# Expert routing spread over the units of the shared expert, and layer-norm moments taken one batch ahead, in a two-layer attention and expert kernel

## Chip, cores and metric

One core of one Trainium2 chip. The metric is the time of one execution in microseconds on the device; the kernel before has a median of 3525.72 us over 3 runs (3525.45 to 3530.16).

## What is computed

The input `x` is 8 batches of 512 tokens of 256 numbers (4096 tokens in all). Each of two layers adds a cross attention and an expert layer to it:

```python
x = x + L0_xattn(_layernorm(x), ctx)
x = x + L0_ffn(_layernorm(x))            # 16 routed experts of 128, 1 shared expert
x = x + L1_xattn(ctx, _layernorm(x))
x = x + L1_ffn(_layernorm(x))            # 8 routed experts of 352, a shared expert of 2 x 352
# L0 choice of experts
scores = sigmoid(x @ gate_w.T); c = scores + e_bias
group_scores = top_k(c.reshape(T, 4, 4), 2).sum(-1)      # the best 2 of 4 groups stay
topk_idx = top_k(where(group kept, c, 0), 4)
w = scores[topk_idx]; w = w / (w.sum(-1) + 1e-20) * 2.5
# L1 choice
scores = softmax(x @ gate_w.T); w, i = top_k(scores, 2); w = w / (w.sum(-1) + 1e-20) * 2.5
# each expert e: y += w_e * (silu(x @ Wg_e) * (x @ Wu_e)) @ Wd_e ; the shared expert has weight 1
```

## The kernel before, in words

All engines run in order through a list of stages; between two stages stands a barrier of all engines. The residual `res` stays in SBUF. The stages, with their place in the profiled span: layer-0 attention (first its norms and transposes, 0 to 57 us, then its heads, to 261); logits and choice of layer 0 (261 to 338); experts of layer 0 (339 to 920); keys and attention of layer 1 (to 2837); logits and choice of layer 1 (2837 to 2896); slot plan (2897 to 2917); first half of layer 1's shared expert, named `ea` (2918 to 3054); routed blocks (3055 to 3381); second half of the shared expert, `eb` (3383 to the end).

**Norm and logits** (`moe_routes`, L546). For each of 8 batches VectorE runs `ln_vector` (L96): four `bn_stats`, four `bn_aggr`, the variance plus eps; it waits for ScalarE's square root, takes the reciprocal and writes four tiles `xh`. TensorE turns `xh` into PSUM `px`; ScalarE copies it to `xs` and rounds it into the high part of `XH`; GpSimd subtracts for the low part; TensorE multiplies `xs` with the gate weights into `pl`. TensorE turns batch b+1 before it does the logits of batch b. `ln_vector` of batch b+1 comes whole after that of batch b. The first stage of attention 0 uses the same `ln_vector`, for batch b+1, ahead of the copy of `px` of batch b (L195 to L199); there ScalarE's queue has the square root of b+1 (`ln_scalar`, L115) ahead of its copy of the context `cT`, after which GpSimd loads a further context tile, and SyncE loads batch b+2 of `x` once `xh` of batch b is written.

**Choice** (`route0` L696, `route1` L1042). When all logits are there, VectorE alone works: it ranks the experts of each token by comparing each pair (`chosen`, L657: for each distance d a comparison, an addition and a subtraction), takes those of low rank and weighs them into `Wt` (`weigh`, L677). In layer 1 a plan follows as a stage of its own (`layer1_plan`, L1098): two small matmuls count the tokens of each expert, VectorE works out a slot for each token and choice (`slot`), and the expert of each block (`bexp`).

**Experts** (`moe_experts`, L764). The work is a row of units: one unit is one batch and one piece of up to 128 of an expert's inner width. In layer 0 there are 17 experts of 8 units, in `ea` and `eb` 24 units (three pieces for each batch). Unit u: TensorE does `gate_up` (12 matmuls into `pG` and `pU`, L855), ScalarE the silu (L907), VectorE the product `mult` (L956), ScalarE rounds it to `hs` high (L910), GpSimd subtracts for `hs` low (L935), TensorE does `down` (12 matmuls, L871), and after a batch's last piece VectorE adds the result, times the token's weight, to `res` (`add`, four instructions, L965). TensorE's order is gate_up(u+1), down(u); VectorE's is mult(u+1), add(u). `pG` and `pU` have two buffers: gate_up(u+2) waits for mult(u). In layer 0 the loop runs over pairs of experts, 0 to 15, then the shared expert comes as expert 16, written out. In `ea` GpSimd also issues, after each unit's subtraction, three indirect DMAs that send the tokens' rows to their slots (`Dispatch`, L1188): 64 in all, so in units 0 to 21. The stage ends when all of them have landed.

Of the kernel before, what the change touches and what calls it, by code (L numbers as in the profile page):

```python
# [6 lines left out]
P = 128  # L7
B, S, D = 8, 512, 256
TPB = S // P
# [86 lines left out]
def ln_vector(dve, s, n, src, st, mv, ve, rs, dst):  # L96

    for t in range(TPB):
        dve.bn_stats(st[:, t, :], src(t)).then_inc(s["stats"], 1)
    dve.wait_ge(s["stats"], n * TPB + TPB)  # L100
    dve.memset(ve[:, :], 0.0).then_inc(s["cleared"], 1)
    for t in range(TPB):
        dve.bn_aggr(mv[:, t, :], st[:, t, :]).then_inc(s["moments"], 1)
    dve.wait_ge(s["moments"], n * TPB + TPB)
    dve.wait_ge(s["cleared"], n + 1)
    dve.tensor_scalar(ve[:, :], mv[:, :, 1], EPS, None, ALU.add).then_inc(s["var"], 1)
    dve.wait_ge(s["sd"], n + 1)
    dve.reciprocal(rs[:, :], ve[:, :]).then_inc(s["rstd"], 1)
    dve.wait_ge(s["rstd"], n + 1)
    for t in range(TPB):  # L110
        dve.tensor_scalar(dst(t), src(t), mv[:, t, 0:1], rs[:, t:t + 1], ALU.subtract,
                          ALU.mult).then_inc(s["xhat"], 1)


def ln_scalar(act, s, n, ve):  # L115
    act.wait_ge(s["var"], n + 1)
    act.activation(ve[:, :], ve[:, :], ACT.Sqrt).then_inc(s["sd"], 1)
# [14 lines left out]
def layer0_attention(nc, io, res, ident):  # L132
    with ExitStack() as ctx:
# [5 lines left out]
        with ExitStack() as inner:  # L139
# [4 lines left out]
            st = sb1("a_st", [P, TPB, 6])  # L144
            mv = sb1("a_mv", [P, TPB, 2])
            ve = sb1("a_ve", [P, TPB])
            rs = sb1("a_rs", [P, TPB])
# [7 lines left out]
            with nc.Block() as block:  # L155
# [30 lines left out]
                def _(dve):  # L186
                    for k in range(2):
                        dve.memset(ahead[:, k:k + 1], 0.0).then_inc(x_out, 1)
                    def normalise(b, i, k):
                        dve.wait_ge(x_in[k], 16 * i + 16)  # L190

                        ln_vector(dve, ls, b, lambda t: res[:, bass.ds(b * TPB + t, 1), :].rearrange(
                            "p a d -> p (a d)"), st, mv, ve, rs, lambda t: xh[:, k, t, :])

                    def emit(b, i, k):  # L195
                        if not (isinstance(b, int) and b == B - 1):
# [4 lines left out]
                    normalise(0, 0, 0)  # L201
# [3 lines left out]
                def _(act):  # L205
                    for k in range(2):
                        act.copy(ahead[:, 2 + k:3 + k], ident[:, 0:1]).then_inc(c_out, 1)
                    def emit(b, i, k):
                        if not (isinstance(b, int) and b == B - 1):
                            ln_scalar(act, ls, b + 1, ve)  # L210
# [3 lines left out]
                    ln_scalar(act, ls, 0, ve)  # L214
# [331 lines left out]
def moe_routes(nc, io, res, ident, XH, Wt, tag, E, route, rows=None):  # L546


    with ExitStack() as ctx:
# [4 lines left out]
        st = sb(f"{tag}_st", [P, TPB, 6])  # L554
        mv = sb(f"{tag}_mv", [P, TPB, 2])
        ve = sb(f"{tag}_ve", [P, TPB])
        rs = sb(f"{tag}_rs", [P, TPB])
# [7 lines left out]
        r = route(nc, io, sb, sem, pl, Wt, logits_done, tag)  # L565

        with nc.Block() as block:
            @block.sync
            def _(sp):
                sp.dma_start(gate[:, :, :], io[f"{tag}_gate"]).then_inc(gate_in, 16)  # L570
                r["sync"](sp)

            @block.vector
            def _(dve):
                def emit(b, i, k):
                    if not (isinstance(b, int) and b < 2):
                        dve.wait_ge(turned, b - 1)
                    ln_vector(dve, ls, b, lambda t: res[:, bass.ds(b * TPB + t, 1), :].rearrange(
                        "p a d -> p (a d)"), st, mv, ve, rs, lambda t: xh[:, k, t, :])

                for_batches(dve, emit)
                r["vector"](dve)

            @block.gpsimd
            def _(pool):
                r["gpsimd_first"](pool)
# [12 lines left out]
            def _(act):  # L599
# [3 lines left out]
                def emit(b, i, k):  # L603
                    if not (isinstance(b, int) and b == B - 1):
                        ln_scalar(act, ls, b + 1, ve)
# [9 lines left out]
                ln_scalar(act, ls, 0, ve)  # L615
                for_batches(act, emit)
                r["scalar"](act)
# [39 lines left out]
def chosen(dve, c, v, E, top, beats, rank, sel):  # L657

    v3, r3 = (x.rearrange("p (g e) -> p g e", e=E) for x in (v, rank))


    for e in range(E):
        n = c.done(dve.memset(r3[:, :, e:e + 1], float(E - 1 - e)))
    G = v3.shape[1]
    for d in range(1, E):
# [1502 lines left out]
```

## Time and profile before

| | |
|---|---|
| runs, median (lowest, highest) | 3525.72 us (3525.45, 3530.16) |
| the profiled execution's own time | 3523.55 us |
| its span, first to last instruction | 3522.0 us |
| busy in the span: TensorE, VectorE | 3188.7 us (91%), 2037.6 us (58%) |
| busy: ScalarE, GpSimd | 1273.8 us (36%), 1626.9 us (46%) |
| mean granted TensorE clock | 0.945 of full speed |

PE is TensorE, PEld its weight loads, DVE VectorE, ACT ScalarE, POOL GpSimd, SP SyncE; a q behind a name is that engine's queue of instructions, which issues DMAs and waits. The stages follow each other, so each has its own limit, and a busy share over the whole span says little of one stage.

### The profile page before, as it was taken

To read this page: it belongs to the slowest core of one execution; us is meant where nothing else is said; L and a number is where in the kernel's file an instruction comes from. 1 tells how busy PE (TensorE), PEld (TensorE's weight loads), DVE (VectorE), ACT (ScalarE), POOL (GpSimd) and SP (SyncE) were. 2 spreads that over 40 slices of the span, in tenths; PEclk is the share of its full clock that TensorE was granted. 3 is DMA by queue.
4 is the path that set the end of the run, shared out by engine and by line. 5 is a ranking of instruction groups with operands and counts; after the bars stand their busy time and mean duration, and the time that the engine had idled before them with its cause. 6 is when DMAs were issued, how large, how long until landed. Compare 5 with 4: busy or idle time off the path is not lost. (4 is left out here: it accounts for less than half of the span.)

```text
span 3522.0 us, 56185 instructions
## 1 busy us (share of the span) xinstructions
PE 3188.7 (91%) x17981; PEld 2290.7 (65%) x17982; DVE 2037.6 (58%) x4470; ACT 1273.8 (36%) x1786; POOL 1626.9 (46%) x933
## 2 busy tenths in 40 slices
PE   5875999999539999999999999999999957699988
PEld 4655888888536666666666666666666555477766
DVE  5656555555746666666766766666666662122235
ACT  2332333333434444444444444444444432122222
POOL 5002333333235666655666655666656636500037
PEclk8995999999769999999999999999999958899999
DMA  4000000001451111111111101111010031421223
GB/s 110 1 1 9 14 13 9 13 9 57 162 214 46 52 45 46 53 45 35 61 45 54 45 27 69 45 54 45 27 69 28 7 106 64 140 68 63 63 70 109
DMA packets 89978, 192.94 MB, mean 55 GB/s; under 512 B 12768, under 2 KB 58152, under 8 KB 83760
## 3 DMA queue, kind: packets, MB, share of 16 engines
q1 hardware_dynamic: 74864, 162.28, 13.1%
q0 software_dynamic: 10816, 21.07, 2.1%
q10 hardware_dynamic: 4224, 8.65, 0.7%
q8 instruction: 40, 0.66, 0.1%
q14 instruction: 34, 0.28, 0.0%
HBM read 137.60 MB, written 54.30 MB: 54 GB/s over the span
## 5 line engine op out<-in xcount | busy, mean ns | idle before, releaser
L2070 POOL TENSOR_TENSOR d_acc<-d_acc,d_pr 128x1024 f32<-128x1024 f32 x384 | 938.2, 2443 | 91.1 <-ACT d_pr L1974 60.4
L1974 ACT ACTIVATE d_pr<-d_p 128x1024 f32<-128x1024 f32 x512 | 487.0, 1026 | 236.2 <-PE d_p L1909 236.2
L1843 PE MATMUL d_pO<-d_pr,d_V 128*64 128x512 f32 x2048 | 473.0, 599 | 0.0
L2070 POOL TENSOR_TENSOR d_acc<-d_pr 128x1024 f32<-128x1024 f32 x64 | 153.1, 2392 | 620.9 <-ACT d_pr L1974 620.9
L2019 DVE TENSOR_REDUCE d_nm<-d_p 128x2 f32<-128x1024 f32 x256 | 304.6, 1222 | 94.9 <-PE d_p L1886 94.9
L2014 DVE CUSTOM_DVE_ANT_0 d_biased<-d_p,d_masked 128x512 f32<-128x512 f32 x512 | 330.6, 688 | 31.8 <-issue 31.8
L935 POOL TENSOR_TENSOR e_hs<-e_hf,e_hs 128x512 fp32r<-128x512 f32 x136 | 175.6, 1291 | 365.4 <-ACT e_hs L910 365.4
L1843 PEld LDWEIGHTS d_pO<-d_pr,d_V 128*64 128x64 f32 x2048 | 135.4, 136 | 261.5 <-issue 235.0
L965 DVE SCALAR_TENSOR_TENSOR res<-e_pY,m_Wt,res 128x256 f32<-128x256 f32 x544 | 225.9, 478 | 44.6 <-PE e_pY L871 43.8
L2030 DVE RECIPROCAL d_rb<-d_rb 128x128 f32<-128x128 f32 x256 | 224.6, 920 | 7.5 <-ACT d_rb L1967 7.5
L871 PEld LDWEIGHTS e_pY<-e_Wd,e_hs 128*128 128x128 f32 x1632 | 213.5, 191 | 13.8 <-POOL e_hs L935 2.2
L871 PE MATMUL e_pY<-e_Wd,e_hs 128*128 128x256 f32 x1632 | 217.2, 283 | 2.7 <-POOL e_hs L935 2.7
L855 PE MATMUL e_pG<-m_XH,e_Wgu 128*128 128x512 f32 x816 | 212.1, 395 | 3.6 <-issue 3.6
L956 DVE TENSOR_TENSOR e_hf<-e_sl,e_pU 128x512 f32<-128x512 f32 x136 | 93.7, 689 | 208.9 <-ACT e_sl L907 208.9
L1886 PE MATMUL d_p<-d_KH,d_QH 64*128 64x512 f32 x1024 | 208.1, 443 | 5.4 <-DVE d_nm L2014 2.5
L1886 PEld LDWEIGHTS d_p<-d_KH,d_QH 64*128 64x128 f32 x1024 | 88.8, 184 | 190.3 <-issue 127.9
L1959 ACT COPY d_V<-d_p 128x1024 f32<-128x1024 f32 x64 | 64.8, 1012 | 400.1 <-PE d_p L1874 400.1
L1909 PE MATMUL d_p<-d_QM,d_KM 64*128 64x512 f32 x1024 | 208.3, 402 | 0.2 <-ACT d_pr L1974 0.2
L855 PE MATMUL e_pU<-m_XH,e_Wgu 128*128 128x512 f32 x816 | 208.3, 391 | 0.0
L1909 PE MATMUL d_p<-d_QH,d_KL 64*128 64x512 f32 x1024 | 202.3, 390 | 0.0
L1909 PE MATMUL d_p<-d_QL,d_KH 64*128 64x512 f32 x1024 | 202.0, 389 | 0.0
L1909 PE MATMUL d_p<-d_QH,d_KH 64*128 64x512 f32 x1024 | 201.6, 388 | 0.0
(287 smaller groups left out, 5628.2 us busy)
## 6 DMA issues: line engine op xcount, KB each, us to landing
d_W<-w_split SPq DMA_DIRECT2D x32, 1536.0 KB, 6.4
kv_split<-c_ys SPq DMA_DIRECT2D x16, 1024.0 KB, 5.7
d_kv<-kv_split SPq DMA_DIRECT2D x8, 2048.0 KB, 10.6
d_masked<-mask_bias SPq DMA_DIRECT2D x64, 256.0 KB
x_slots<-m_zeros SPq DMA_DIRECT2D x1, 9088.0 KB, 29.7
b_x<-x_slots SPq DMA_DIRECT2D x71, 128.0 KB, 2.0
y_slots<-b_y SPq DMA_DIRECT2D x71, 128.0 KB, 1.7
w_split<-w_parts SPq DMA_DIRECT2D x4, 1536.0 KB, 5.3
```

The lines of the kernel that those rows point to most:

```text
L855: last = pe.matmul(out[u % 2][0:fw, :], lhsT, XH[:, xp, k, n * S:(n + 1) * S], start=start, stop=(k == DC - 1 and (wp, xp) == PASSES[-1]))
L871: last = pe.matmul(pY[n % 2][:, t, :], hs[0:fw, u % 2, hp, t * P:(t + 1) * P], Wd[j][0:fw, wp, f, :], start=(f == 0 and m == 0 and t % 2 = ...
L935: pool.tensor_tensor(hs[0:fw, u % 2, LO, :], hf[0:fw, u % 2, :], hs[0:fw, u % 2, HI, :].bitcast(F32), ALU.subtract).then_inc(lo_done, 1)
L965: dve.scalar_tensor_tensor(res[:, tile, :], pY[n % 2][:, t, :], Wt[:, tile, bass.ds(e + column, 1)], res[:, tile, :], ALU.mult, ALU.add).t ...
L1843: last = pe.matmul(pO[own[h], :], V[vb][:, s, par * P + h * HD1:par * P + (h + 1) * HD1], pr[:, s % PT, h, :], start=(s == 0), stop=(s == ...
L1886: last = pe.matmul(out[:, h, :], QH[j][own[h], qt * P:(qt + 1) * P], KH[j][own[h], m * S:(m + 1) * S], start=True, stop=True)
L1909: last = pe.matmul(out[:, h, :], k_[own[h], s * P:(s + 1) * P], q_[own[h], :], start=(i == 0), stop=(i == len(terms) - 1))
L1974: act.activation(pr[:, n % PT, :, :], slot(st, what, n)[:, :, :], ACT.Exp).then_inc(exp_done, 1)
L2014: dve.tensor_tensor_reduce(biased[:, h, :], out[:, h, :], masked[j][:, :], -1.0, MASKED, ALU.add, ALU.min, nm2[:, j, h * TPB + qt, m:m + 1 ...
L2019: dve.tensor_reduce(both, out[:, :, :], AX.X, ALU.max, negate=True).then_inc(max_done, 1)
L2030: dve.reciprocal(rb[:, quarter], rb[:, quarter]).then_inc(r_done, 1)
L2070: pool.tensor_tensor(acc[:, q, :, :], a, pr[:, s % PT, :, :], ALU.add).then_inc(acc_done, 1)
```

## The change

Four edits.

1. **Norms.** `ln_vector` is split into `ln_moments` (to the variance) and `ln_apply` (reciprocal and tiles), with two buffers. In both logits stages VectorE takes the moments of batch b+1 ahead of the application to batch b. In attention 0 the order is: moments of b+1, copy of `px` of b, application to b+1.
2. **Choice of layer 0.** The logits stage ends with the sigmoid. The experts' stage begins with the shared expert (`last_first`), written out, and behind each of its 8 units VectorE runs one piece of the ranking; the weights are done after unit 7. The loop then runs over the routed experts.
3. **Choice and plan of layer 1.** The logits stage ends with a copy of the logits to SBUF. Choice and plan stand as eleven pieces behind units 0 to 10 of `ea`. The exponential is run by ScalarE behind unit 1, the counts by TensorE behind unit 4, in the `pG` and `pU` buffers of that unit; gate_up(6), which writes these next, waits until they are read. The stage of the plan is gone.
4. **`ea`.** The low part of `hs` is made by VectorE, ahead of `mult` (`low_on_vector`). GpSimd waits once for the slots, which are there after unit 8, and issues the 64 indirect DMAs; its list has no other wait.

The core of the diff (`chosen` is cut into `rank_begin`, `rank_steps` and `rank_end` with the same instructions):

```diff
-def ln_vector(dve, s, n, src, st, mv, ve, rs, dst):
+def ln_moments(dve, s, n, k, src, st, mv, ve):
     (bn_stats, memset, bn_aggr, variance + EPS, as before, in buffer k)
+def ln_apply(dve, s, n, k, src, mv, ve, rs, dst):
     dve.wait_ge(s["sd"], n + 1)
     (reciprocal and the four tiles, as before, from buffer k)
@@ attention 0, VectorE
-                            normalise(b + 1, i + k, 1 - k)
+                            moments(b + 1, i + k, 1 - k)
                         dve.wait_ge(x_turned, b + 1)
                         dve.tensor_copy(xT[:, :, bass.ds(b * S, S)], px[k][:, :, :]).then_inc(x_out, 1)
+                        if more:
+                            apply(b + 1, 1 - k)
@@ moe_routes, now moe_logits, VectorE
                 def emit(b, i, k):
+                    if not (isinstance(b, int) and b == B - 1):
+                        ln_moments(dve, ls, b + 1, 1 - k, tile_of(b + 1), st, mv, ve)
                     if not (isinstance(b, int) and b < 2):
                         dve.wait_ge(turned, b - 1)
-                    ln_vector(...)
+                    ln_apply(dve, ls, b, k, tile_of(b), mv, ve, rs, lambda t: xh[:, k, t, :])
+                ln_moments(dve, ls, 0, 0, tile_of(0), st, mv, ve)
                 for_batches(dve, emit)
-                r["vector"](dve)
@@ ScalarE, end of the stage
+                act.wait_ge(logits_done, B + 2)
+                route.take_logits(act, pl)
@@ moe_experts
-        tail = NX % 2 or 2
-        loops = (NX - tail) // 2
+        tail = (NX - 1) % 2 or 2
+        loops = (NX - 1 - tail) // 2
         def for_units(eng, emit):
+            for u in range(UPE):
+                emit(0, 0, u, NX == 1 and u == UPE - 1)
@@ TensorE: in gate_up, and behind down
+                    if isinstance(e, int) and e == 0:
+                        beside.spare_read(pe, u)
+                        beside.first_tensor(pe, u, (pG[u % 2], pU[u % 2]))
@@ GpSimd
-                    pool.wait_ge(hi_done, U + 1)
-                    pool.tensor_tensor(hs[0:fw, u % 2, LO, :], ...)
+                    if not low_on_vector:
+                        pool.wait_ge(hi_done, U + 1)
+                        pool.tensor_tensor(hs[0:fw, u % 2, LO, :], ...)
@@ VectorE
                 def emit(e, j, u, last):
+                    if low_on_vector:
+                        low(e, u)
                     if not last:
                         mult(*next_pair(e, j, u))
                     if u % NF == NF - 1:
                         add(e, u // NF)
                     beside.vector(...)
+                    if isinstance(e, int) and e == 0:
+                        beside.first_vector(dve, u, (pG[u % 2], pU[u % 2]))
@@ Route0.first_vector
+        if u == 0:     (bias, pair sums, their maximum, rank_begin of the groups)
+        elif u == 1:   (rank of the groups, mask, rank_begin)
+        elif u < B - 1:
+            ds = {2: range(1, 3), 3: range(3, 5), 4: range(5, 8), 5: range(8, 11), 6: range(11, E0)}[u]
+            rank_steps(dve, self.c, self.ch[:, :], self.rank[:, :], E0, self.beats, ds)
+        else:          (rank_end, weigh)
@@ Route1
+    SEND_FROM, SEND = 11, 5
+    COUNT_AT = 4
+    def take_logits(self, act, pl):
+        act.copy(self.lg[:, :], pl[:, :, :].rearrange("p t e -> p (t e)")).then_inc(self.taken, 1)
+    def first_tensor(self, pe, u, spare):
+        if u == self.COUNT_AT:
+            pe.wait_ge(self.pick_ready, 1)
+            (the two matmuls of the counts, into spare)
+    def spare_read(self, pe, u):
+        if u == self.COUNT_AT + 2:
+            pe.wait_ge(self.counts_read, 1)
+    def first_scalar(self, act, u):
+        if u == 1:
+            act.wait_ge(self.shifted, 1)
+            act.activation(self.lg[:, :], self.lg[:, :], ACT.Exp).then_inc(self.exp_done, 1)
+    def first_vector(self, dve, u, spare):
+        0: maximum, subtraction, constants   1: softmax, distances 1, 2   2: distances 3 to 7
+        3: rank_end, picked, weigh   4: counts, prefix sums   5: places, blocks of each expert
+        6: starts, number of the choice   7, 8: slot and weight of choice 0, 1 (slot_ready)
+        9, 10: expert of each block
+    def gpsimd(self, pool, u):
+        if u == self.SEND_FROM:
+            pool.wait_ge(self.slot_ready, 2)
+        if u >= self.SEND_FROM:
+            for _ in range(min(self.SEND, NT * TOPK1 - self.sent)):
+                (one indirect DMA, as before)
```

## Rows read from the trace of the kernel before

**Rows 1.** Windows by stage: start:end, us, busy (instructions) by engine, PEclk, DMA share, GB/s.
```profile
262.00:308.00 46.00, 40.90 (x196) 40.31 (x196) 31.74 (x119) 20.06 (x27) 19.95 (x16) 0.52 0.01 1
308.00:338.00 30.00, 0.00 (x0) 0.00 (x0) 27.61 (x89) 0.48 (x1) 0.00 (x0) 0.50 0.00 0
88.00:240.00 152.00, 134.72 (x562) 93.24 (x560) 97.95 (x174) 51.07 (x89) 0.00 (x0) 1.00 0.00 1
240.00:260.00 20.00, 12.78 (x40) 7.39 (x40) 7.04 (x14) 4.19 (x7) 0.00 (x0) 0.83 0.00 0
```

**Rows 2.** Timeline, logits stage of layer 0: start, duration, engine, line, operation, count [idle before].
```profile
261.40 1.41 DVE L99 BATCH_NORM_STATS2 m_st<-res 128x6 f32<-128x256 f32 x4 [0.92 <-PEq L86]
263.92 1.38 DVE L111 TENSOR_SCALAR m_xh<-res,m_mv,m_rs 128x256 f32<-128x256 f32 x4
...
269.16 1.97 PE L632 MATMUL m_px<-ident,m_xh 128*128 128x128 f32 x8 [1.82 <-DVE m_xh L111]
...
299.26 1.95 PE L632 MATMUL m_px<-ident,m_xh 128*128 128x128 f32 x8
...
301.00 6.85 PE L642 MATMUL m_pl<-m_gate,m_xs 128*128 128x16 f32 x32
```

**Rows 3.** Timeline, VectorE: first instruction of the choice of layer 0, first of its experts.
```profile
308.51 0.69 DVE L719 TENSOR_TENSOR m_ch<-m_sg,m_ebias 128x512 f32<-128x512 f32 x1 [11.31 <-ACT m_sg L713]
...
339.04 0.09 DVE L946 MEMSET e_ahead<- 128x1 f32 x2 [1.07 <-PEq L86]
```

**Rows 4.** Windows over what becomes pieces 0 and 7 of 8, layer 0.
```profile
308.50:311.60 3.10, 0.00 (x0) 0.00 (x0) 2.92 (x7) 0.00 (x0) 0.00 (x0) 0.50 0.00 0
...
334.54:338.00 3.46, 0.00 (x0) 0.00 (x0) 3.18 (x8) 0.00 (x0) 0.00 (x0) 0.50 0.00 0
```

**Rows 5.** Timeline, VectorE in the experts of layer 0: mult, add, mult.
```profile
357.83 0.69 DVE L956 TENSOR_TENSOR e_hf<-e_sl,e_pU 128x512 f32<-128x512 f32 x1 [1.50 <-ACT e_sl L907]
...
358.85 1.66 DVE L965 SCALAR_TENSOR_TENSOR res<-e_pY,m_Wt,res 128x256 f32<-128x256 f32 x4 [0.33 <-PE e_pY L871]
...
362.01 0.69 DVE L956 TENSOR_TENSOR e_hf<-e_sl,e_pU 128x512 f32<-128x512 f32 x1 [1.50 <-ACT e_sl L907]
```

**Rows 6.** Timeline, logits stage of layer 1: a GpSimd subtraction and a VectorE instruction beside it.
```profile
2846.84 2.50 POOL L594 TENSOR_TENSOR m_XH<-m_xs,m_XH 128x512 f32 x2 [8.89 <-ACT m_XH L613]
...
2847.16 0.97 DVE L106 TENSOR_SCALAR m_ve<-m_mv 128x4 f32<-128x4 f32 x1
```

**Rows 7.** Timeline, layer 1: table load, first instruction of the choice, first of `ea`.
```profile
2880.64 1.28 ACT L1063 ACT_TABLE_LOAD   x1
...
2884.21 0.42 DVE L1069 TENSOR_REDUCE m_tot<-m_pl 128x32 f32<-128x256 f32 x1 [9.60 <-PE m_pl L642]
...
2918.11 0.09 DVE L946 MEMSET ea_ahead<- 128x1 f32 x2 [1.18 <-PEq L86]
```

**Rows 8.** Window over what becomes piece 2 of layer 1.
```profile
2889.47:2893.44 3.97, 0.00 (x0) 0.00 (x0) 3.59 (x16) 0.00 (x0) 0.00 (x0) 0.50 0.00 0
```

**Rows 9.** Timeline, `ea`: second mult, two sends, the last send, first load of the blocks.
```profile
2936.16 0.69 DVE L956 TENSOR_TENSOR ea_hf<-ea_sl,ea_pU 128x512 f32<-128x512 f32 x1 [2.48 <-ACT ea_sl L907]
...
2961.05 0.99 POOL L1188 DMA_INDIRECT x_slots<-m_rows,m_slot  x1 [0.17 <-issue]
...
2962.34 0.97 POOL L1188 DMA_INDIRECT x_slots<-m_rows,m_slot  x1 [0.30 <-issue]
...
3041.27 0.99 POOL L1188 DMA_INDIRECT x_slots<-m_rows,m_slot  x1 [0.17 <-issue]
...
3055.65 28.95 SPq L1296 DMA_DIRECT2D b_x<-x_slots  x5
```

**Rows 10.** Timeline, first stage: load of batch 4, its first use, the last copy.
```profile
21.22 0.41 SPq L159 DMA_DIRECT2D res<-in_x_dram  x1
...
29.11 1.41 DVE L99 BATCH_NORM_STATS2 a_st<-res 128x6 f32 x4 [2.05 <-DMA res<-in_x_dram]
...
54.87 1.23 DVE L199 COPY a_xT<-a_px 128x1024 f32<-128x1024 f32 x1 [3.82 <-PE a_px L233]
```

More of the change, by code:

```diff
@@ L654, in over, with rank_begin, rank_steps @@
     return a.rearrange("p (o m) -> p o m", o=1).to_broadcast([P, n, a.shape[1]])
-def chosen(dve, c, v, E, top, beats, rank, sel):
+def rank_begin(dve, c, rank, E):
+    r3 = rank.rearrange("p (g e) -> p g e", e=E)
+    for e in range(E):
+        c.done(dve.memset(r3[:, :, e:e + 1], float(E - 1 - e)))
+def rank_steps(dve, c, v, rank, E, beats, ds):
     v3, r3 = (x.rearrange("p (g e) -> p g e", e=E) for x in (v, rank))
-    for e in range(E):
-        n = c.done(dve.memset(r3[:, :, e:e + 1], float(E - 1 - e)))
     G = v3.shape[1]
-    for d in range(1, E):
+    for d in ds:
+        dve.wait_ge(c.sem, c.now())
         b3 = beats[d % 2][:, 0:G * (E - d)].rearrange("p (g e) -> p g e", e=E - d)
@@ L689, in weigh @@
     dve.wait_ge(c.sem, n)
-    c.done(dve.memset(Wt[:, :, E:E + shared], 1.0))
     n = c.done(dve.tensor_tensor(Wt[:, :, 0:E], sel.rearrange("p (t e) -> p t e", e=E), over(tot, E, "last"),
@@ L912, in emit @@
                         split(e + 1, (j + 1) % 2)
+                    if isinstance(e, int) and e == 0:
+                        beside.first_scalar(act, u)
                     if isinstance(e, int) and e == NX - 1:
@@ new lines, in __init__ @@
+        TE = NT * E1
+        self.Wt, self.rows, self.slot, self.wk, self.bexp, self.xslots = Wt, rows, slot, wk, bexp, xslots
+        self.sent = 0
+        self.zeros = sb("m1_zeros", [P, D])
+        self.lg, self.sel, self.rank = (sb(f"m1_{n}", [P, TE]) for n in ("lg", "sel", "rank"))
+        self.beats = [sb(f"m1_beats{k}", [P, TE]) for k in range(2)]
+        self.total = sb("m1_tot", [P, NT])
+        self.upper = sb("s_upper", [P, P])
+        self.ones = sb("s_ones", [P, P])
+        self.order_i = sb("s_order_i", [P, NBLK], mybir.dt.int32)
@@ new lines, in __init__ @@
+        self.order_f = sb("s_order_f", [P, NBLK])
+        self.thr = sb("s_thr", [P, NT])
+        self.picked, self.tot, self.run, self.run2, self.place, self.mk = (
+            sb(f"s_{n}", [P, TE]) for n in ("picked", "tot", "run", "run2", "place", "mk"))
+        self.nblk, self.bs, self.bs2, self.start = (sb(f"s_{n}", [P, E1]) for n in ("nblk", "bs", "bs2", "start"))
+        self.bf = sb("s_bf", [P, NBLK])
+        self.slot_f = sb("s_slot_f", [P, TOPK1, NT])
+        (self.zeros_ready, self.slots_cleared, self.set_up, self.taken, self.shifted, self.exp_done, self.consts,
+         self.pick_ready, self.counted, self.counts_read, self.slot_ready, self.scattered, self.steps) = (
+             sem(f"s_{n}") for n in ("zeros_ready", "slots_cleared", "set_up", "taken", "shifted", "exp_done", "consts",
+                                     "pick_ready", "counted", "counts_read", "slot_ready", "scattered", "steps"))
@@ new lines, in before_vector, with take_logits, first_tensor @@
+    def before_vector(self, dve):
+        dve.memset(self.Wt[:, :, E1:E1 + NS1], 1.0).then_inc(self.set_up, 1)
+    def take_logits(self, act, pl):
+        act.copy(self.lg[:, :], pl[:, :, :].rearrange("p t e -> p (t e)")).then_inc(self.taken, 1)
+    COUNT_AT = 4
+    def first_tensor(self, pe, u, spare):
+        if u == self.COUNT_AT:
+            pe.wait_ge(self.pick_ready, 1)
+            for out, left in zip(spare, (self.upper, self.ones)):
+                pe.matmul(out[:, 0:NT * E1], left[:, :], self.picked[:, :], start=True, stop=True
+                          ).then_inc(self.counted, 1)
```

409 lines of the change are left out of this document (205 added, 204 removed).

## Prediction

> **What bounds the kernel now.** I read the windows by stage first. Where TensorE has work it is busy, but the two choices are holes: in 308 to 338 us it does nothing and VectorE works alone, 27.61 of 30 us [rows 1]. The timeline then gives the holes' edges: in layer 0 from the choice's first instruction (308.51) to the experts' first (339.04), 30.5 us [rows 3]; in layer 1 from 2884.21 to 2918.11, 33.9 us, plan and two barriers within [rows 7]. In the logits stages TensorE sets the pace: its turns come each (299.26 - 269.16)/6 = 5.02 us, and 40.9 of 46 us are busy, at a granted clock of 0.52 [rows 1, 2]. In layer 0's experts a unit takes 362.01 - 357.83 = 4.18 us; VectorE needs 0.69 + 1.66 = 2.35 of it, so 1.8 is free [rows 5]. In `ea` a unit takes (3041.27 - 2961.05)/16 = 5.01 us: three sends of 0.97 and a pause of 0.30 each on GpSimd, and a subtraction in the rest, 1.2, without a gap [rows 9]. There GpSimd bounds.
>
> **Choice of layer 0.** The stage now ends with the sigmoid, which ended at 308.5; a barrier takes 1.07 [rows 3]. The experts start at 309.6, 29.5 us earlier. The same instructions now stand behind the units: eight pieces, from 3.1 to 4.4 us, 29.5 together: the stretch between the edges without its barrier [rows 3], first and last of the eight in [rows 4]. VectorE's list per unit becomes 2.35 + 3.7 = 6.05 us against TensorE's 4.18. It is strictly in order and mult(u+2) stands behind piece u; gate_up(u+4) waits for that mult. So here VectorE bounds. Without the pieces mult(2) to mult(9) take 7 x 4.18 = 29.3 us. With them mult(2) waits for piece 0, some 2 us after its old place of 357.83, and each further cycle is piece + 2.4: the pieces of units 1 to 7 (26.4) and 7 x 2.4 = 16.8 bring mult(9) to 45.2 us after the old mult(2). Delay 45.2 - 29.3 = 16. TensorE's buffers give back almost nothing, since down(9) waits for the same mult. Added to this: VectorE's ranking reads two SBUF tiles, and a GpSimd subtraction of 1.3 us falls into each unit. A VectorE instruction that takes 0.17 elsewhere took 0.97 beside GpSimd, to the end of the first of two subtractions [rows 6]. Bounds per unit 0 and 1.3 us; most of the subtraction falls beside `add`, so I take 0.25, 2 us in all. Net: -29.5 + 16 + 2 = **-11.5**.
>
> The Trainium skill ("SBUF — State Buffer", on the shared port pair) says that a VectorE instruction with two SBUF inputs and a GpSimd instruction take an exclusive lock, and the loser waits to the other's end. By that rule alone, with no overlap by `add`, the 8 units would lose 8 x 1.3 = 10 us; the trace agrees that the wait ends with the other's end [rows 6].
>
> **Norms.** In the logits stages both engines' work stays, only the start differs. Moments take 2.0 us (263.92 - 261.40 less 0.5 for root and reciprocal), the application 1.6 [rows 2]. Batch 1's tiles are now there after three moments and two applications, 6.0 + 3.2 = 9.2: 270.6, against 269.1 before (turn(1) began at 269.16, waiting for VectorE). From there TensorE is never late, so 1.5 us stay, in both layers: **+3**. Bounds: 0, and a gain of 6 us per stage if TensorE should get its full clock and VectorE's list (3.9) be the pace.
> In attention 0 the order gets worse. Application b+1 stands behind the copy that waits for the turn of b. So ScalarE's root, and behind it the copy of the context, come an application (1.6 us) later, and the context load behind that; and `x` of batch b+2 is asked for later. That load takes 29.11 - 21.22 = 7.9 us and its user already waits 2.05 for it [rows 10]. The cycle over two batches becomes load 7.9, moments 2.0, copy 1.2, application 1.6 = 12.7. The first such application ends at 18.7 (turn of batch 0 to 15.9, copy 1.2, application 1.6); three cycles give 56.8, then turn and copy 3.2: 60, against 54.87 + 1.23 = 56.1 before, the stage's last copy [rows 10]. I take **+3**; bounds -1 (the roots' waits of 0.5 go) and +7.
>
> **Choice and plan of layer 1.** A copy of 0.42 us and one barrier replace 33.9 us: `ea` starts at 2885.75, 32.3 us earlier [rows 7]. All times now with this shift. Two mults are done at 2904.5 (2936.16 + 0.69 - 32.3) [rows 9]. Then VectorE's list up to the end of piece 8:
> - pieces 0 to 8: 1.85 + 24.1 = 26.0 (3.6, 3.97, 2.7, 3.6, 2.4, 2.7, 2.6, 2.6 for pieces 1 to 8, cut from the same stretch; the dearest, piece 2, in [rows 8]);
> - eight low parts of 0.73 and eight mults of 0.73: 11.7. No row shows the low part on VectorE; the nearest is the mult, 0.69; bounds 0.6 and 1.3 (GpSimd's time);
> - three adds, 5.0, and before each 0.75 for the down that the low part has just released: 2.2;
> - silu(2) behind an exponential that stands between two table loads of 1.28 [rows 7]: 1.6 late;
> - piece 4 waits for down(4) and the two count matmuls: 1.9; while they are read gate_up(6) waits, 0.1 more.
> Sum 48.5: the slots are there at 2953.0. TensorE (4.18 a unit) would then be through with all 24 units at about 3017. But GpSimd only now begins 64 sends of 1.27 = 81.7 us, and needs to 3034.7. So the sends set the end, 18 us behind TensorE. The last lands 2 us later, a barrier takes 2: first load of the blocks at 3038.7 against 3055.65 [rows 9]: -17. VectorE's low parts, two SBUF inputs each, run beside 19 units of sends; a send may be held by one (0 to 0.7 us per unit, 0 to 13 in all). I take 2: **-15**. What is late next is thus the DMA issue, not the plan. The idle TensorE starts the blocks at half clock, but it waits there for weights anyway.
>
> The pieces 9 and 10 (3 us) and the constants on GpSimd (0.8 us, now in the logits stage beside idle GpSimd) cost nothing: 14 units of slack on VectorE, and GpSimd is busy 19.95 of 46 us in a logits stage [rows 1]. The clearing of `x_slots` by SyncE and its loads stay where they were. The written-out units change no instruction's duration.
>
> **Sum.** +3 (attention 0) - 11.5 + 1.5 (layer 0) - 15 + 1.5 (layer 1) = -20.5. Profiled execution: 3523.55 - 20.5 = 3503; it lies 2.2 under the median, so **3505** for the median of the runs.
>
> **Rivals.**
> (a) *TensorE's clock falls in the VectorE-bound units.* Its busy share there is 4.18/6.1 = 0.68 in layer 0, about 0.75 in `ea`. Against it: 88 to 240 us stays at 1.00 with 0.89 busy. For it: in 240 to 260, at 0.64 busy with gaps of some us, the clock went to 0.83, both of the two levels (2.4 and 1.2 GHz) within [rows 1]. If it fell to 1.2 GHz, a unit costs 8.4: layer 0 loses 8 x 2.3 = 18, `ea` up to slot 8 some 20, and that goes through to the sends. 3505 + 38 = 3543. It decides in this direction as soon as half of these 17 units are slow. The Trainium skill ("TensorE: Matmul & The Clock Gate", HAM oscillation) speaks for it: the low rate is the default, and matmuls with waits between them fall back again and again.
> (b) *The two engines hinder each other.* Each subtraction stops a ranking instruction whole (+8 in layer 0), each low part a send (+11): 3505 + 19 = 3524, no change.
> (c) *The norms gain.* TensorE gets full clock in the logits stages, since tiles come evenly; 6 us each instead of losses of 1.5, and attention 0 at 0: 3505 - 18 = 3487. Against it: TensorE is busy all through there and yet at 0.52.
> (d) *The sends are quicker than 1.27 us back to back*, 0.97 without the pause: 64 x 0.3 = 19 us less, `ea` ends with TensorE: 3487. Against it: the pause of 0.30 stands within each burst of three.
>
> **Chances.** Forecast 0.64 (own range 3496 to 3516), (a) 0.09, (b) 0.13, (c) 0.08, (d) 0.06. The range that holds 8 in 10: from 3491 to 3523; the low end takes in part of (c), the high end most of (b). A difference of 0.2%, 7 us, is about what this measurement can tell from none. Faster (below 3518.7): 0.62 + 0.08 + 0.06 + 0.04 of (b) and 0.02 of half an (a) = 0.82. Same: 0.02 + 0.08 = 0.10. Slower: 0.08.
>
> **What would show it.** In layer 0 the first unit starts 25 us earlier than before (29.5 less the norms' 4.5); in units 1 to 7 mults 5.8 to 6.8 us apart; from unit 9 on 4.18; the lead at the end of layer 0's experts some 7 us. In `ea`: no send before 2950, then 64 at 1.27 to 1.35 us; TensorE finished 15 to 20 us before the last; a VectorE queue without a gap in units 1 to 8. First matmul of the blocks 20 us earlier than before. I am wrong if the granted clock in the first units is under 0.9, if VectorE's instructions there are longer than in the rows, if the sends do not end last in `ea`, or if the first stage is not longer.

## The result, and the profile after

| | before | after |
|---|---|---|
| runs, median (lowest, highest) | 3525.96 us (3525.45, 3530.16) | 3562.8 us (3560.84, 3566.9) |
| profiled execution: own time, span | 3523.55, 3522.0 | 3560.84, 3559.2 |
| mean granted TensorE clock | 0.945 | 0.939 |

The change makes the kernel slower by 37 us: ratio 1.0107, 95% interval 1.0096 to 1.0119. The forecast was 3505, faster.

The edges of the stages say where. This is the timeline of the kernel after, at the places of [rows 10, 2, 3, 5, 7, 9]: last copy of the first stage, start of the logits stage, second turn there, first instruction of layer 0's experts, mult(9) and two later mults, first instruction of `ea`, first and last send, first load of the blocks.

```profile
58.27 1.23 DVE L209 COPY a_xT<-a_px 128x1024 f32<-128x1024 f32 x1 [2.02 <-PE a_px L246]
...
266.01 0.42 DVE L99 BATCH_NORM_STATS2 m_st<-res 128x6 f32<-128x256 f32 x1 [0.96 <-PEq L86]
...
274.94 1.97 PE L650 MATMUL m_px<-ident,m_xh 128*128 128x128 f32 x8 [1.45 <-DVE m_xh L115]
...
315.10 0.09 DVE L955 MEMSET e_ahead<- 128x1 f32 x2 [12.38 <-PEq L86]
...
380.55 0.69 DVE L965 TENSOR_TENSOR e_hf<-e_sl,e_pU 128x512 f32<-128x512 f32 x1 [0.32 <-DVE m_Wt L715]
...
392.82 0.69 DVE L965 TENSOR_TENSOR e_hf<-e_sl,e_pU 128x512 f32<-128x512 f32 x1 [1.56 <-ACT e_sl L913]
...
397.06 0.69 DVE L965 TENSOR_TENSOR e_hf<-e_sl,e_pU 128x512 f32<-128x512 f32 x1 [1.56 <-ACT e_sl L913]
...
2887.88 0.09 DVE L955 MEMSET ea_ahead<- 128x1 f32 x2 [11.09 <-PEq L86]
...
2957.20 1.26 POOL L1277 DMA_INDIRECT x_slots<-m_rows,m_slot  x1 [58.65 <-DVE m_slot L1260]
...
3038.19 0.97 POOL L1277 DMA_INDIRECT x_slots<-m_rows,m_slot  x1 [0.30 <-issue]
...
3094.53 27.37 SPq L1385 DMA_DIRECT2D b_x<-x_slots  x5
```

Differences of the edges, after less before, in us:

| stretch | forecast | measured |
|---|---|---|
| to the end of attention 0 (266.01 - 261.40) | +3 | +4.6, 3.4 of it in the first stage |
| logits stage 0, to the second turn (274.94 - 269.16, less 4.6) | +1.5 | +1.2 |
| choice of layer 0, to mult(9) (380.55 - 387.09, less 5.8) | -11.5 | -12.3 |
| rest of layer 0's experts (923.34 - 922.23, less -6.5) | 0 | +7.6 |
| attention 1 | 0 | +0.1 |
| logits stage 1 with its choice, to `ea` (2887.88 - 2918.11, less 1.2) | -30.8 | -31.4 |
| `ea` to the first load of the blocks: 206.65 against 137.54 | +17.3 (154.9) | **+69.1** |
| blocks and `eb`, to the end | 0 | -1.6 |
| sum | -20.5 | +37.3 |

One row carries the loss. Its windows in the kernel after: up to the standstill, and the standstill.

```profile
2905.00:2974.00 69.00, 55.62 (x286) 44.63 (x284) 45.80 (x136) 16.72 (x26) 12.92 (x13) 0.95 0.07 24
2975.00:3040.00 65.00, 12.63 (x39) 9.28 (x40) 3.64 (x7) 1.21 (x2) 48.92 (x51) 0.53 0.29 103
```

For 65 us TensorE, VectorE and ScalarE do nearly nothing, while GpSimd sends. The timeline inside it (x is a count, in brackets the idle time before and its releaser):

```profile
2984.33 1.66 DVE L974 SCALAR_TENSOR_TENSOR res<-ea_pY,m_Wt,res 128x256 f32<-128x256 f32 x4 [10.72 <-remote]
...
3016.53 0.60 ACT L913 ACTIVATE ea_sl<-ea_pG 128x512 f32<-128x512 f32 x1 [42.27 <-remote]
...
3034.74 0.58 PE L859 MATMUL ea_pG<-m_XH,ea_Wgu 128*128 128x512 f32 x1 [2.22 <-issue]
...
3037.54 0.58 PE L859 MATMUL ea_pG<-m_XH,ea_Wgu 128*128 128x512 f32 x1 [2.22 <-issue]
```

The matmuls of one `gate_up` have no wait between them, and yet come 2.8 us apart; no row of another engine releases them. VectorE's addition at 2984.33 takes the result of matmuls that had ended at 2969.2, and ScalarE's silu at 3016.53 that of matmuls that had ended at 2972.0. So each of the three engines stands with its inputs ready. The DMA view has queues of kind "instruction". Over 2966 to 3058 the one that I take for TensorE's has three fetches (0.05 MB) in the kernel before, and none of them has any in the kernel after. The first line is of the kernel before, the second, the only queue left, of the kernel after:

```profile
q8 instruction: 3, 0.05, 0.2%
```
```profile
q0 software_dynamic: 2786, 7.61, 23.3%
```

Narrow windows of that view (3 us each) date TensorE's fetches of about 16 KB: before 2937, 2961, 2991, 3015, 3042; after 2937, 2964, and then 3060. A unit of `ea` is 48 instructions on TensorE. The Trainium skill ("Runtime: NRT & Kernel Launch", Instruction fetch mechanics) says that each engine's sequencer fetches blocks of 16 KiB, 256 instructions, by its own DMA queue, and that this is mostly hidden. The size agrees with the rows.

I took this for engines without instructions, and the expectations below call it that. Counting TensorE's work between two fetches speaks against it. The first two windows are of the kernel after: from the last fetch ahead of the standstill to the next one, and the end of that stretch. The third is of experiment 1, which has no standstill, between the two fetches at the same place:

```profile
2965.07:3061.53 96.46, 35.82 (x132) 26.65 (x131) 11.93 (x25) 6.45 (x11) 56.64 (x58) 0.59 0.23 80
3045.20:3061.53 16.33, 15.08 (x55) 11.26 (x55) 5.61 (x10) 3.54 (x6) 0.00 (x0) 0.65 0.00 0
```
```profile
2970.23:2993.86 23.63, 23.63 (x132) 19.63 (x131) 12.38 (x24) 6.51 (x11) 19.76 (x21) 1.00 0.23 80
```

TensorE ran 132 matmuls between the two fetches with the standstill and 132 without it. In the kernel after it had been at work again for 16 us, 55 matmuls, when the next fetch came. So that fetch came at its usual place in TensorE's list, and its absence during the standstill can be an effect of the standstill as well as its cause. A second queue of this kind has fetches of 8 KB; experiment 1 has none of them between 2952 and 3072, and nothing stands there. What the experiments below show is which sends make the engines stand. By what way they do it stays open.

### The profile page after: what moved, and what is told of

It reads as the page before. It is cut to its first block and busy times, and to the rows that moved or that the text cites. A ratio compares the mean times of both kernels' runs of the same rounds, so it can differ in the third digit from the quotient of the medians.

```text
span 3559.2 us, 56051 instructions
## 1 busy us (share of the span) xinstructions
PE 3211.7 (90%) x17981; PEld 2304.7 (65%) x17982; DVE 2069.1 (58%) x4495; ACT 1265.2 (36%) x1781; POOL 1596.6 (45%) x909
## 5 line engine op out<-in xcount | busy, mean ns | idle before, releaser
L875 PEld LDWEIGHTS e_pY<-e_Wd,e_hs 128*128 128x128 f32 x1632 | 215.9, 193 | 30.8 <-POOL e_hs L944 14.8
```

The source lines that it names most:

```text
L875: last = pe.matmul(pY[n % 2][:, t, :], hs[0:fw, u % 2, hp, t * P:(t + 1) * P], Wd[j][0:fw, wp, f, :], start=(f == 0 and m == 0 and t % 2 = ...
```

## The experiments

All were timed against the kernel before on the same chip; times are medians, and the ratio is to that kernel, whose medians beside them were 3525.0 to 3528.2 us.

**1. A pause behind every third send.** GpSimd in the kernel before had a subtraction between bursts of three sends [rows 9]; the change moved it to VectorE, and with it went the only pause.

```diff
+                if self.sent % 3 == 0:
+                    pool.memset(self.gap[:, :], 0.0)   # 128x1024
```

> The kernel after, with a fill of 128x1024 on GpSimd (about 0.95 us) behind every third send; nothing else is changed. Theory (instruction supply): in the kernel after, TensorE, VectorE and ScalarE stand still from 2975 to 3040 us because the fetch of their next instructions, which travels by DMA, does not get through while 64 sends follow each other with 0.3 us between them; the kernel before left 1.45 us of GpSimd work between bursts of three sends and stood nowhere. Then the gaps cure it: the units go on at 4.2 to 5 us, the last send goes out at about 3038 + 21 x 1.1 = 3061, the units are done before it, the first block load follows at about 3065 instead of 3094.5, and the whole takes 3533 (3527 to 3540). Rival (port): VectorE, which has the low parts now, and GpSimd hinder each other at their common port; then a few more GpSimd instructions change nothing or cost: 3562 to 3585. Rival (send bandwidth): the bytes of the sends fill the DMA engines; the rate falls only by a fifth, so most of the standstill stays: 3550 to 3565.

3536.8 us, 1.0035 (1.0021 to 1.0049). The window of the same stretch, and the fetches are back (2968, 2992, 3016):

```profile
2963.00:3024.00 61.00, 59.56 (x336) 50.30 (x335) 28.16 (x55) 16.43 (x27) 51.09 (x52) 0.97 0.24 85
```

TensorE is busy 59.56 of 61 us, though GpSimd has more to do than before and VectorE as much. The rival of the port falls, and so does that of the send bandwidth, which had most of the standstill stay. The run does not say whether a lack of instructions or something else held the engines.

**2. No sends at all.**

> The kernel after, with each of the 64 sends replaced by a fill of 128x1024 on GpSimd (about 0.95 us, one after the other, as long as a send's own row of 0.97): rows are not dispatched, so the blocks work on zeros. Theory (instruction supply): without DMAs nothing keeps the fetches out, the units never stop, the last of them ends at about 2972 + 14 x 4.25 = 3032, the blocks' first load follows at about 3034 instead of 3094.5: 3502 (3495 to 3510). Rival (port): GpSimd is as busy beside VectorE's low parts as before, so the standstill from 2975 to 3040 stays at least in half: 3530 or more.

3498.1 us, 0.9919 (0.9902 to 0.9936): the standstill is gone (TensorE busy 58.98 of 61 us over 2963 to 3024) with GpSimd as busy (54.06). The DMAs make it.

**3. That part of the change alone, on the kernel before:** `low_on_vector=True` for `ea`, nothing else.

> The kernel before with one part of the change alone: in layer 1's first shared expert the low parts are made on VectorE, so that GpSimd has nothing but the sends. Choice, plan, norms, addresses stay as before. Theory (instruction supply): the sends follow each other without a pause from 2936 to 3018; the engines run out of instructions some 17 us after the first send, as in the kernel after (2957 to 2974), with four or five of the 24 units done, stand until 3020, and then need 19 or 20 units of 4.24 us: the first block load goes from 3055.65 to about 3105, and the whole takes 3574 (3560 to 3582). Rival (the new choice in pieces, not the sends, is what costs): without it the units are only quicker (4.24 us instead of 5.01, the sends done at 3018): 3500 to 3512.

3578.2 us, 1.0151 (1.0134 to 1.0168). The same standstill, without the choice in pieces; its rival falls:

```profile
2956.00:2990.00 34.00, 13.45 (x44) 9.23 (x42) 1.38 (x2) 1.22 (x2) 25.77 (x28) 0.60 0.29 101
2990.00:3018.00 28.00, 2.35 (x4) 1.16 (x4) 0.00 (x0) 0.00 (x0) 19.06 (x20) 0.50 0.27 97
```

So moving the low parts off GpSimd is by itself enough for the loss.

**4. How much pause?** Short fills behind every third send, long ones behind every sixth, short ones behind each, and bursts of 21.

> As e1_gaps, with a third of the gap: the fill behind every third send is 128x256 (0.31 us by its row) instead of 128x1024 (0.97). It asks how long the pause has to be. Theory A (the fetch only needs one moment without a send behind it): the standstill stays away, the last send goes out at about 3038 + 21 x 0.45 = 3048, the first block load follows 9 us later as in e1_gaps, at 3057: 3525 (3519 to 3532). Theory B (the fetch moves only as far as the pause lasts): a third of the pause leaves the engines starved for part of the time: 3537 to 3560. The port has no part in it under either.

3563.3 us: nothing is cured. Theory A falls, and theory B's range was too low as well.

> As e1_gaps, with the gap of 0.97 us behind every sixth send instead of every third. TensorE's fetches come 24 us apart in e1_gaps, so one pause in 8.6 us is enough if one pause lets a whole fetch through: last send at about 3038 + 10 x 1.1 = 3049, first block load at 3058, 3526 (3520 to 3532). If a fetch needs several pauses one after the other, or its transfers are spread over the pauses, half as many pauses leave part of the standstill: 3535 to 3555.

3534.6 us (10 runs, 3523.2 to 3541.2), between the two ranges. One pause in 8.6 us was not enough: the next fetch comes at 3004 instead of 2992 and `ea`'s last add at 3068 instead of 3024; in 2990 to 3020 TensorE is busy 18.8 of 30 us. Half a cure, and the sends end 9 us earlier.

> As e5_gap_short (fill of 0.31 us), but behind every send instead of every third: the free share of the time is about that of e1_gaps, in short pieces. Theory C (the share decides): no standstill, 64 x 1.75 = 112 us of sends, the last at 3069, first block load at 3078, 3546 (3538 to 3552). Theory D (a pause must have some length, more than 0.31 us): nothing gets through for 112 us, the units go on only at 3069, first block load at 3124, 3592 (3580 to 3600).

3529.2 us, 1.0008 (0.9998 to 1.0018): cured, with pauses no longer than in e5. Theory D falls. Theory C's time was 17 us too high, since the sends took 1.486 us each, not 1.75: the pause of 0.30 within a burst shrinks to 0.16 beside a fill.

> The kernel after with a fill of 128x128 (0.2 us by its row in the profile) behind every send: one send in about 1.36 us, 96 GB/s, evenly spread. Theory M: above the 92 GB/s at which part of the standstill was there, so the engines stop as in the kernel after: last send at 3043, units end at about 3096, 3563 (3550 to 3570). Theory P (any pause behind each send lets the fetch through, as with 0.31 us): no standstill, first block load at 3052, 3520 (3512 to 3527).

3559.8 us, 1.0088 (1.0071 to 1.0104): not cured, with a pause behind every send; TensorE's fetches come at 2971 and 3058. Theory P falls here. Fetches are not kept out altogether: over 3018 to 3056, where TensorE is busy 0.59 of 38 us and the sends go on to 3053, the view has one of the second queue.

```profile
q14 instruction: 1, 0.01, 0.1%
```

> The kernel after with five fills of 0.97 us behind every 21st send and no pause otherwise: bursts of 27 us with 5.6 us between them, mean rate 131 KB / 1.54 us = 85 GB/s. Theory M (a backlog that grows with the mean rate above some 90 GB/s): in 27 us at 102 GB/s against 90 the backlog grows by 27 x 12% = 3 us of writes, which delays a fetch by a few us and empties in the pause; the units of the shared expert end at 3024 to 3032, the last send goes out at 3038 + 3 x 5.6 = 3055, 3532 (3526 to 3538). Theory P (a fetch needs a pause to start in, and waits for the next one): fetches wait up to 27 us, the engines stand for part of each burst, the units end after 3045, and the whole takes 3540 to 3560.

3540.9 us (3533.9 to 3546.8): the low end of theory P's range. TensorE is busy 14.93 of 28 us in a burst (2997 to 3025). Its matmuls resume at 2994.1 and 3022.4, with the sends' pauses, which begin at 2990.8 and 3022.4. The fetch, however, did not wait for a pause as theory P has it: it came at 3029.7, when the sends had gone on for 2 us. So a low mean does not help when a burst of 27 us is above the limit. What fits these five is that the rate held over some ten to twenty us decides, not that there is a pause.

**5. What about a send does it?** Plain DMAs of the same rows from SyncE, from GpSimd, from GpSimd at the pace of the sends; indirect sends to slots in order; indirect sends of half rows.

```diff
-                pool.indirect_dma_start(self.xslots, bass.IndirectOffsetOnAxis(self.slot[:, k, t:t + 1], 0), ...
+                pool.dma_start(self.xslots[self.sent * P:(self.sent + 1) * P, :], ...          # e11, e13
+                pool.indirect_dma_start(self.xslots, bass.IndirectOffsetOnAxis(self.line[:, ...   # e14
```

> The kernel after, with the 64 indirect sends of GpSimd replaced by 64 plain DMAs of the same rows (128 x 1 KB each) that SyncE issues back to back once the slots are ready, to consecutive slots: the rows are not permuted, so the blocks work on other rows than they should. The bytes are the same, GpSimd and its queue are out of it. Theory 1 (it is GpSimd's queue that keeps the fetches out): no standstill, the units end at 3024 as in e1_gaps, and the first block load follows at 3025 to 3045: 3492 to 3512, middle 3500. Theory 2 (any dense stream of DMAs does): the engines stop while the 8.4 MB move, at the 215 GB/s of the weights' loads for 39 us, at 103 GB/s for 81: 3525 to 3560.

3491.4 us, no standstill at 262 GB/s: TensorE is busy 19.00 of 19 us over 2975 to 2994, and the sends run to 2992.5. Theory 2 falls.

> The kernel after with the 64 indirect sends replaced by 64 plain DMAs of the same rows that GpSimd itself issues back to back, to consecutive slots (the rows are not permuted). It parts the engine that issues from the queue that carries: in the profile before, plain DMAs of GpSimd run on a hardware queue (q10), the indirect ones on the software queue (q0). Theory 1 (the software queue keeps the fetches out): no standstill, 3491 as with SyncE issuing, 3485 to 3500. Theory 3 (whatever GpSimd issues in a dense row does): the standstill stays, 3530 to 3563.

3490.1 us. The time is that of theory 1, its reason is wrong: the plain DMAs ran on the software queue too (its 3072 packets are on `q0`), at 245 GB/s, and stopped nothing. It is not the queue.

> As e11_plain_from_gpsimd (64 plain DMAs of the rows by GpSimd, not permuted), but each followed by a fill of 128x704 on GpSimd (about 0.67 us), so that they come about 1.3 us apart, as the indirect sends do, for 83 us instead of 34. Theory I (it is the indirect form that keeps the fetches out): no standstill, the last DMA at about 3042, the first block load at 3050, 3520 (3510 to 3528). Theory R (a stream of some 80 us at this pace does it, and the plain ones were only over too soon): standstill as in the kernel after, 3550 to 3570.

3532.2 us: no standstill. They came 1.54 us apart instead of 1.3, which makes the 12 us over the forecast and leaves 85 GB/s, so alone it would not settle theory R.

> The kernel after with the 64 indirect sends as they are, but with slots counted up (row p of send m goes to slot 128 m + p) in place of the chosen ones: the rows are not permuted. Theory S (it is the scattered addresses in memory): no standstill, last send at 3038, first block load at 3047, 3515 (3508 to 3522). Theory I (the indirect instruction itself, whatever its addresses): all as in the kernel after, 3563 (3556 to 3570).

3518.9 us, 0.998 (0.9971 to 0.999): cured, with the same instruction, at the same 1.29 us (TensorE is busy 46.43 of 49 us over 2975 to 3024). The addresses do it.

> The kernel after with indirect sends of half a row each (128 x 512 B instead of 128 x 1 KB; only the first half of each row is dispatched). Theory B (the bytes in flight keep the fetches out): half the bytes leave half the time free: no standstill or a short one, 3515 to 3530. Theory I (what GpSimd does for an indirect DMA, the same for half rows): the send still takes 0.97 us by its row and the standstill stays, 3563 (3556 to 3570).

3517.9 us: cured, at the same 0.97 us of GpSimd per send, with addresses scattered as before and half the bytes. Theory I falls in both: it takes scattered rows and enough bytes.

The runs in one table (rate: 131,072 bytes by the mean distance of the starts of the 64 sends):

| sends | rate, GB/s | standstill |
|---|---|---|
| scattered rows of 1 KB: before, e4, e8, e1 | 78, 78, 83, 83 | none |
| e12, e15, e10 | 87.4, 88.2, 88.3 | none |
| e6 | 91.8 | half |
| e18, e5, e9, after, e3 | 94.7, 96.8, 101, 102, 102 | whole |
| e17: mean 86, in bursts of 27 us at 102 | 86 | in each burst |
| scattered half rows of 512 B (e16) | 51 | none |
| rows of 1 KB in order: e13, e14, e11, e7 | 85, 101, 245, 262 | none |

The DMA engines themselves are not full: they are busy 0.29 of the standstill in the kernel after (the window above), 0.28 over 2975 to 3024 in e14, and 0.79 over 2975 to 2994 in e7, where nothing stands. In e8, e10 and e12 (below) the sends go in another order, all of the first choice and then all of the second, so among the runs near the limit e15 is the one with the order of the kernel after.

**6. Addresses and norms.** Layer 0's experts lie 17,088 bytes higher in the kernel after, since the choice's tensors stay alive below them. The weights' addresses then leave 96 by 128 instead of 32. One run undoes this with 64 unused bytes, and the norms; the other does both to the kernel before.

```diff
+        pad = sb("m0_pad", [P, 16])
         moe_experts(nc, io, res, ident, XH, Wt, "e0", N0, I0, ...
```

> The kernel after with two edits in stages that do not meet: the norms of attention 0 and of both logits stages in the order of before (moments and scaling of a batch together), and 64 unused bytes per partition ahead of the tensors of layer 0's experts, so that their addresses leave the same rest by 128 as in the kernel before (32 instead of 96). Theory: the norms' new order costs 4.6 us up to the end of attention 0 and 1.2 in layer 0's logits stage, which come back; the up matmuls of layer 0's experts go back from 397 to 391 ns and the unit from 4.24 to 4.18 us, because it is the address that slows them: 127 x 0.06 = 7.6 us. Together 13.4 us, and perhaps 1 in layer 1's logits stage: 3549 (3546 to 3552). Rival (code): the unit is slower because of the written-out first expert or the other order of the two weight buffers in the loop: it stays at 4.24, and the whole is 3556. The standstill beside the sends stays under both.

> The mirror of the run above: the kernel before with the new order of the norms (moments one batch ahead, in attention 0 and in both logits stages) and with 64 unused bytes per partition ahead of the tensors of layer 0's experts (addresses leave 96 by 128 as in the kernel after). Choice and slot plan stay as before. Theory: first stage and attention 0 end 4.6 us later, logits 0 another 1.2, the unit of layer 0's experts takes 4.24 instead of 4.18 us, 136 x 0.06 = 8: 3526 + 14 = 3540 (3536 to 3543). Rival (code): the unit stays at 4.18: 3532. Rival (the norms gain once nothing else is changed): 3522 or less, or with the slow unit 3530.

3550.5 us (1.0068, 1.0051 to 1.0085) and 3539.0 us (1.0041, 1.0027 to 1.0056). The up matmuls over 600 to 727.2 us: before, after, e3, e4.

```profile
L855 PE MATMUL e_pU<-m_XH,e_Wgu 128*128 128x512 f32 x180 | 45.7, 389 | 0.0
```
```profile
L859 PE MATMUL e_pU<-m_XH,e_Wgu 128*128 128x512 f32 x180 | 46.9, 397 | 0.0
```
```profile
L856 PE MATMUL e_pU<-m_XH,e_Wgu 128*128 128x512 f32 x186 | 47.2, 389 | 0.0
```
```profile
L873 PE MATMUL e_pU<-m_XH,e_Wgu 128*128 128x512 f32 x180 | 46.8, 394 | 0.0
```

The unit goes 4.18, 4.24, 4.18, 4.23 us. 64 bytes make and unmake it; the written-out expert has no part. In e4 attention 0 ends at 265.58, 4.2 later than before [rows 2], in e3 at 263.52, 2.5 earlier than in the kernel after. The norms' new order gains nowhere. Its cost in the first stage stands clear: the last copy starts at 50.7 to 54.9 us in the six profiled runs with the old order and at 56.9 to 59.3 in the fourteen with the new. The end of attention 0 spreads more, 257.4 to 265.5 and 263.7 to 269.4, so what lies behind the first stage is not told from chance.

**7. A version meant to gain.** Pauses, aligned addresses, the norms of before, and the first pieces of both choices ahead of mult(0), where VectorE waits 9.3 and 13.2 us for weights in the kernel after.

```diff
                 beside.ahead_vector(dve)     # 2 of 8 pieces in layer 0, 4 of 11 in layer 1
                 mult(0, 0, 0)
```

> A version meant to gain: e3_norms_back_aligned, plus the gaps of e1_gaps, plus the first pieces of both choices (2 of 8 in layer 0, 4 of 11 in layer 1) moved ahead of the first unit's multiplication, where VectorE waits 9.3 and 13.2 us for the weights in the kernel after; the choices' other pieces follow at the units from 0 on, and the sends of the first choice start when its slots are there. Theory: layer 0's units are held by VectorE two units less, 8 us off the 590 of its experts, so that its stage ends 15 to 18 us earlier than in the kernel before; in layer 1 the slots are ready at about 2938 instead of 2957 (times of the kernel after), the last send goes out at 3037 to 3040, the first block load at about 3048: 9 us earlier than before. Together 3501 (3494 to 3508). Rival: VectorE's pieces in a row run on TensorE's cold start and the units behind them are later by as much as the pieces take: 3512 to 3518. If the standstill comes back: 3535 and more.

3489.6 us, 0.9889 (0.9873 to 0.9906). First send at 2918.4, first load of the blocks at 3027.1 against 3055.65 [rows 9]. The first send goes out 39 us earlier than in the kernel after: 11.6 us of that come from the stages ahead (`ea` starts at 2876.26), the rest from pieces that fill the wait for weights, and from the first choice's sends not waiting for the second's slots. The forecast, 3501, had that 20 us too small. Two with less pause:

> As e8_early_pieces with shorter pauses: the fill behind every third send is 128x640 (about 0.6 us) instead of 128x1024 (0.97). Theory C (the share of the time that is left free decides): full cure at 0.97 us in 4.95 us (20%), half a cure at 0.97 in 8.8 (11%), none at 0.31 in 4.3 (7%); 0.6 in 4.6 is 13%, a part of the standstill comes back: 3488 to 3505. Theory D (a single pause must reach a length between 0.31 and 0.97, and 0.6 is enough): the last send goes out 21 x 0.37 = 8 us sooner and nothing stalls: 3482 (3479 to 3486).

> As e8_early_pieces with the pause of 0.97 us behind every fourth send. By theory C the free share is 0.97 in 6.2 us (16%), between the full cure (20%) and the half (11%): up to 10 us of standstill against 6 us of pauses saved, 3484 to 3495. By theory D the length is the same as in e8_early_pieces and only the number of pauses falls, from 21 to 16: the last send goes out 5 x 1.1 = 5.5 us sooner: 3484 (3481 to 3488), unless a fetch of 24 us finds too few pauses, which six in a row showed and four would show less.

3486.4 us (0.989, 0.9873 to 0.9906) and 3485.9 us (0.9887, 0.987 to 0.9903). Both stay under 89 GB/s and show no standstill; they are not told apart from e8. The first falls between the ranges of its two theories, the second within both. The best is 40 us faster than the kernel before.

## Why the prediction was wrong

- **Choice of layer 0: right.** -12.3 against -11.5, first unit 23.9 us earlier (25 forecast), VectorE bound in units 1 to 7. The waits beside GpSimd were there: a piece's first ranking instruction, of 480 elements, took 1.03 us beside a subtraction, the next of the same size 0.66.
- **Norms: right in kind,** +1.2 for +1.5 in the logits stage, +4.6 for +3 ahead of it (3.4 of it in the first stage).
- **"The written-out units change no instruction's duration": wrong by 7.6 us,** though not by the writing-out. The change moved the tensors' lifetimes and so the addresses of others; I looked at instructions only. Up matmuls went from 389 to 397 ns, 6 in each of some 127 units, and the gate ones by 5. Undone in e3, made in e4.
- **Slots ready: right.** From `ea`'s start to the first send 69.3 us, 67.3 forecast; 64 sends in 82, forecast 81.7.
- **"TensorE (4.18 a unit) would then be through with all 24 units at about 3017": the failing step.** It took for granted that the units go on beside the sends. I had weighed the sends against VectorE (port) and the end of the stage, and counted GpSimd's subtraction only as time to be saved. It was the pause that kept the sends at 78 GB/s. With 102 TensorE, VectorE and ScalarE stood for 65 us; the first load of the blocks came 56 us after the last send, where the forecast had 4. Experiments 1 to 3 show that the sends do it, e14 and e16 that it takes scattered rows at this rate. Why the engines stand is not shown.
- **The rest of the miss.** e14 has the sends at the forecast pace and no standstill, and takes 3518.9: so 44 us of the 58 between 3562.8 and the forecast are the standstill. Of the other 14 the addresses make 7.6, attention 0 about 1.6, and a mis-sized term the rest: the first load of the blocks comes 9.1 us after the last send in e14, not 4.
- **Rivals.** (a), the clock: 0.94 over 325 to 381 us and 0.95 over 2905 to 2974, the two VectorE-bound stretches; where it fell to 0.53 the engine stood. (b), the port: a few us. (c) and (d): sends stayed at 1.27 us, norms gained nothing. None had engines that stand with their inputs ready beside the sends.

With pauses instead of the standstill the change does not gain either: e1 is slower than before by 0.35%, e15 with shorter pauses is not told from it (1.0008, 0.9998 to 1.0018). The reason is that the choice in pieces has the slots ready at 2957 instead of 2936, and the sends set the end. The forecast gain of 15 us in layer 1 needed 64 sends without a pause, which is just what can't be had with these scattered rows.

## What to carry to other kernels

Before work is moved off an engine that issues scattered DMAs, ask what pace that work kept; here a fill of 0.97 us behind every third send brought 26 us (3562.8 to 3536.8). When engines idle with "issue" or "remote" and their inputs are ready, look at the DMAs of the stretch, and take them out or change their addresses or pace one at a time. Do not take something that is missing from the stretch, here the instruction fetches, for the cause before you have counted the work between two of them. And a tensor that lives longer moves its neighbours: compare a matmul group's mean ns before and after.

## What the runs showed of the hardware

- Scattered writes of 1-KB rows to memory at 94.7 GB/s and more bring TensorE, VectorE and ScalarE nearly to a stand until they end (65 us in the kernel after), while GpSimd goes on with a send each 1.27 us; at 88.3 and less they do not; the same bytes in order do not at 262. The DMA engines are 0.29 busy meanwhile. That writes pile up in the memory behind them fits all runs but was not shown, and neither was what of an engine then waits: a lack of instructions by a way that the recorded fetches do not show, the writing of the records that the profile is made of, or something else. Each timed execution carries its profile, so none tells whether the engines would stand without one. Where between 88.3 and 94.7 the limit lies was not found (e6 at 91.8 stands half).
- TensorE's recorded fetches are of 16 KB and come 117 to 146 matmuls apart in the kernels before and after and in e1, standstill or not.
- The engines do not stop at once: some 17 us from the first send to the standstill (2957 to 2974). Why so long is not shown.
- fp32r matmuls of 512 columns took 389, 394 and 397 ns with the weights' tile 0, 64 and 192 bytes (by 256) away from that of `XH`, the moving operand. Other distances were not tried.
- 64 plain DMAs of GpSimd took 0.54 us each on the engine, on the same queue on which an indirect one takes 0.97.
